# MLP and routing of a half in one stage, with the first choice of experts inside the MLP, and the shared experts inside the first expert stage

## What is computed

```
# layer 1, after the attention
x  = Q + out @ wo + bo
x  = x + gelu(layernorm(x) @ w1 + b1) @ w2 + b2           # MLP, width 512
z  = layernorm(x)                                          # rows for the mixture
scores = sigmoid(z @ gate_w.T)                             # 64 experts in 8 groups of 8
# the best 4 groups by the sum of their two best; in them the best 8 experts
rw = scores of the chosen / (their sum + 1e-20) * 2.5
routed = sum over e of rw[:, e] * mlp_e(z)                 # mlp_e: width 88
shared = (silu(z @ Sg.T) * (z @ Su.T)) @ Sd.T              # width 176 = 2 x 88
x = x + tanh(g_ffn) * (routed + shared)
```

## Time and profile before

| what | us |
|---|---|
| median of three runs | 1210.32 |
| profiled execution | 1209.28 |
| its span | 1207.1 |
| MLP and routing of half 0, about | 196 to 296 |
| MLP and routing of half 1, about | 461 to 554 |
| expert stage 0, TensorE | 554 to 702 |
| TensorE without work | 702 to 727.56 |
| expert stage 1, TensorE | 727.56 to 917 |
| layer 2 | 917 to 1207 |

### The profile page before, as it was taken

How to read it: one execution, slowest core, us unless ns; L and a number is a source line. 1 busy time by engine, 2 the same in 40 slices (tenths; PEclk the granted TensorE clock), 3 DMA queues, 4 the chain that set the end, 5 groups by cost and what they waited for, 6 DMA issues and landing times.

```text
span 1207.1 us, 20571 instructions
## 1 busy us (share of the span) xinstructions
PE 1079.1 (89%) x6232; PEld 742.7 (62%) x6232; DVE 837.1 (69%) x2982; ACT 680.1 (56%) x1192; POOL 539.2 (45%) x544
## 2 busy tenths in 40 slices
PE   5999998875999998778999928998988999999998
PEld 2556665643666665547999917897884444444443
DVE  6888886797888885876444404658665888888643
ACT  3556663342666654334666614556646677767775
POOL 0000000041777772043777777776643777772000
PEclk9999999986999999988999968999989999999999
DMA  9999000000111114005778626666654534554241
GB/s 280 312 285 343 37 1 1 1 1 2 51 53 52 53 54 115 1 1 161 232 245 251 218 88 197 200 197 179 193 161 176 193 93 161 203 202 165 96 161 59
DMA packets 104408, 165.15 MB, mean 137 GB/s; under 512 B 13423, under 2 KB 63063, under 8 KB 99673
## 3 DMA queue, kind: packets, MB, share of 16 engines
q1 hardware_dynamic: 87806, 130.39, 33.2%
q0 software_dynamic: 16512, 33.59, 9.5%
HBM read 94.46 MB, written 69.47 MB: 136 GB/s over the span
## 4 chain that ended last, share of the span: by engine, by line
PE 69%; DVE 19%; POOL 4%; ACT 4%; issue 3%; DMA 1%; SPq 0%; DVEq 0%; ACTq 0%; POOLq 0%
PE PS L1857 8%; PE PS L706 6%; PE PS L1874 6%; PE PS L696 6%; PE PS L1695 5%; PE PS L1685 4%; PE PS L1662 4%; PE PS L1678 4%; PE PS L1657 4%; PE PS L1851 3%; PE PS L1866 3%; PE PS L1670 2%; POOL sorted_rows L945 2%; PE PS L1751 2%; PE PS L1744 2%
## 5 line engine op out<-in xcount | busy, mean ns | idle before, releaser
L964 POOL DMA_INDIRECT sb_Y<-sorted_out,sb_POS x256 | 258.3, 1009 | 114.0 <-issue 68.9
L945 POOL DMA_INDIRECT sorted_rows<-sb_XR,sb_POS x256 | 247.2, 966 | 89.4 <-issue 79.4
L905 POOL TENSOR_TENSOR sb_A<-sb_A 88x512 f32<-88x512 f32 x16 | 21.3, 1349 | 293.3 <-ACT sb_A L1089 293.3
L1857 PE MATMUL PS<-sb_WGU,sb_A 128*128 x768 | 138.4, 324 | 4.6 <-ACT sb_A L1131 4.6
L706 PE MATMUL PS<-sb_A,sb_RT 128*128 128x512 f32 x256 | 131.8, 599 | 4.0 <-DVE sb_A L529 3.9
L1131 ACT ACTIVATE sb_A<-PS 128x512 f32<-128x512 f32 x96 | 57.3, 597 | 130.8 <-PE PS L1851 130.8
L529 DVE SCALAR_TENSOR_TENSOR sb_A<-sb_A,sb_RW 128x512 f32<-128x512 f32 x124 | 85.0, 689 | 60.9 <-ACT sb_A L378 60.3
L1857 PEld LDWEIGHTS PS<-sb_WGU,sb_A 128*128 128x128 f32 x768 | 120.5, 197 | 9.9 <-issue 9.8
L1584 DVE TENSOR_SCALAR sb_A<-PS 128x4 f32<-128x4 f32 x96 | 15.5, 161 | 150.7 <-ACT sb_A L1136 147.8
L696 PE MATMUL PS<-sb_WGU,sb_RT 128*128 128x512 f32 x224 | 115.7, 598 | 0.0
L372 ACT ACTIVATE sb_A<-PS,sb_A 128x512 f32<-128x512 f32 x128 | 87.3, 682 | 41.7 <-PE PS L696 40.6
(11 more groups left out here) (278 smaller groups left out, 2081.8 us busy)
## 6 DMA issues: line engine op xcount, KB each, us to landing
sb_RW<-routing SPq DMA_DIRECT2D x31, 1024.0 KB, 7.6
sorted_rows<-sb_RT SPq DMA_DIRECT2D x2, 12288.0 KB, 77.4
sb_A<-sorted_rows SPq DMA_DIRECT2D x96, 256.0 KB
sorted_out<-sb_A SPq DMA_DIRECT2D x96, 256.0 KB
sb_WGU<-in_wgu SPq DMA_DIRECT2D x1, 5664.0 KB, 60.9
sorted_rows<-sb_XR,sb_POS POOLq DMA_INDIRECT x256
sb_Y<-sorted_out,sb_POS POOLq DMA_INDIRECT x256
sb_RW<-in_wd SPq DMA_DIRECT2D x1, 2816.0 KB
```

Of the source, the lines that this page charges most:

```text
L945: pool.indirect_dma_start(out=xs[c], in_=XR[:, t, :], in_offset=None, out_offset=bass.IndirectOffsetOnAxis(ap=POS[:, b * TOPK + k:b * TOPK ...
L964: pool.indirect_dma_start(out=GBUF[r][:, k * D:(k + 1) * D], out_offset=None, in_=ys[c], in_offset=bass.IndirectOffsetOnAxis(ap=POS[:, b * ...
L1857: ins = mm(gu_bank[r % 2][:, t, 0:1 + 2 * EI], EXT[:, t * P:(t + 1) * P], WGU[:, e[t], :], start=True, stop=True)
```

## The change

On every engine `mlp(c)` and `route(c)` become one function (`ffn(c)` on TensorE and ScalarE, `mlp(c)` on VectorE). The rows of the first two groups are normalised and scored as soon as the MLP has finished with these groups, and their choice (`choose(c, 0)`) stands on VectorE between the MLP's third and fourth group. The scores of two groups leave PSUM by one Sigmoid of 128x512 in place of two of 128x256.

The first pieces of an attention (`begin`: transposes, query and key products and their squares for the first tile) are cut off, and for half 1 they stand inside the stage before. At the start of the kernel the same cut moves ScalarE's first roots behind the squares of the keys and the transposes' eviction of the second tile.

`chosen_scores` of half 0 moves into the attention of half 1; that of half 1 moves into step 1 of expert stage 0. `slot_counts` becomes shorter: its two operations of 128x1024 become operations of 128x64.

The shared experts leave routing and GpSimd. Steps 1 to 40 of expert stage 0 carry them, five steps to a group, eight groups (both halves): four steps with one matmul each, all into the one PSUM bank 7, and a fifth with the sixteen matmuls back into the same bank. ScalarE takes the Silu of the first and third, VectorE the product after the second and fourth, and the addition to `x` after the fifth.

The expert step has another order: `hT`, `T`, the shared matmul, `gu`, `down`. One semaphore (`e_a`) is raised after `hT` and `T`, one (`e_b`, in the listings `ex_gu_y`) after `gu` and `down`. The row's score is no longer folded into the hidden values (one operation of 128x352 in place of four of 128x88), but multiplies the result of `down` as it leaves PSUM, and this eviction (`y_out`) moves from ScalarE to VectorE. The hidden buffers are doubled. SyncE's waits and GpSimd's pace follow the two new semaphores.

GpSimd loses this function, which ran ahead of each half's scatter:

```diff
-            def shared(c):
-                for g in range(c * GC, (c + 1) * GC):
-                    sil, h = SIL[g % 2], SHH[g % 2]
-                    for n in range(2):
-                        pool.wait_ge(r_si, g * 2 + (n + 1))
-                        nc.gpsimd.tensor_tensor(h[:, n, :], sil[:, n, :], h[:, n, :], ALU.mult).then_inc(r_h, 1)
-                    pool.wait_ge(r_oe, g + 1)
-                    xg = X[:, g * G:(g + 1) * G, :]
-                    nc.gpsimd.tensor_tensor(xg, SHO[g % 2].rearrange("p (t d) -> p t d", t=G), xg, ALU.add).then_inc(r_x, 1)
```

Which steps carry shared work, and ScalarE: the cut in its attention, and its share of the shared experts in `experts(c)`:

```diff
+        def shared_step(c, k):
+            n = k - SHARED
+            return divmod(n, 5) if c == 0 and 0 <= n < 5 * (B // G) else None
...
-                qk_in(lo)
-                q_sq(lo)
+                if begin:
+                    if c:
+                        act.wait_ge(m_x, c * GC + 1)
+                    qk_in(lo)
+                    q_sq(lo)
+                    k_sq(lo)
+                    qk_in(lo + 1)
+                    return
                 roots(lo, 0)
-                k_sq(lo)
-                qk_in(lo + 1)
...
+                def shared(k, g, j):
+                    if j % 2 == 0 and j < 4:
+                        act.wait_ge(e_b, b_sig(c, k))
+                        act.wait_ge(r_h, 2 * g + j // 2)
+                        nc.scalar.activation(SIL, bank(7, 1, 0, EI), ACT.Silu).then_inc(r_si, 1)
```

VectorE, in `experts(c)`:

```diff
+                def shared(k, g, j):
+                    if j % 2:
+                        dve.wait_ge(e_b, b_sig(c, k))
+                        dve.wait_ge(r_si, 2 * g + j // 2 + 1)
+                        v.tensor_tensor(SHH[j // 2], SIL, bank(7, 1, 0, EI), ALU.mult).then_inc(r_h, 1)
+                    if j == 4:
+                        dve.wait_ge(e_b, b_sig(c, k))
+                        v.scalar_tensor_tensor(X[:, tiles(g), :], t3(bank(7)), TG[:, 1:2], X[:, tiles(g), :], ALU.mult,
+                                               ALU.add).then_inc(r_x, 1)
+
+                for k in range(-1, SS + 2):
+                    if 0 <= k - 2:
+                        y_out(k - 2)
+                    if k + 1 < SS:
+                        h(k + 1)
+                    if shared_step(c, k):
+                        shared(k, *shared_step(c, k))
+                    if not c and k == 1:
+                        chosen_scores(CHUNKS - 1)
```

TensorE, in `experts(c)`:

```diff
+                def shared(g, j):
+                    if j == 0:
+                        pe.wait_ge(r_x, g)
+                        if g == 0:
+                            pe.wait_ge(t_rout, CHUNKS * NRK)
+                    elif j < 4:
+                        pe.wait_ge(r_si if j % 2 else r_h, 2 * g + (j + 1) // 2)
+                    else:
+                        pe.wait_ge(r_h, 2 * g + 2)
...
+                for k in range(-2, SS + 2):
+                    if k <= SS:
+                        if 0 <= k - 1:
+                            ins = hT(k - 1)
+                        if k + 2 < SS:
+                            ins = T(k + 2)
+                        ins.then_inc(e_a, 1)
+                    if k + 2 < SS:
+                        experts_of[k + 2] = slot_experts(pe, c, k + 2)
+                    if shared_step(c, k):
+                        shared(*shared_step(c, k))
+                    if -1 <= k:
+                        if k + 1 < SS:
+                            ins = gu(k + 1, experts_of[k + 1])
+                        if 0 <= k - 2:
+                            ins = down(k - 2, experts_of.pop(k - 2))
+                        ins.then_inc(e_b, 1)
```

More of the change, by code:

```diff
@@ L236, in build @@
         e_ld = [sem(f"ex_load{i}") for i in range(4)]
-        e_t, e_te, e_gu, e_si, e_h, e_ht, e_hte, e_y, e_ye = (sem("ex_" + n) for n in (
-            "xT", "xT_out", "gu", "silu", "h", "hT", "hT_out", "y", "y_out"))
+        e_a, e_b, e_te, e_si, e_h, e_w, e_hte, e_ye = (sem("ex_" + n) for n in (
+            "xT_hT", "gu_y", "xT_out", "silu", "h", "score", "hT_out", "y_out"))
         e_st = [sem(f"ex_store{i}") for i in range(2)]
@@ L969, in _ @@
             for c in range(CHUNKS):
-                shared(c)
                 scatter(c)
@@ L981, in _, with attention @@
             nc.scalar.activation(TG[:], VEC[:, V_GATES:V_GATES + 4], ACT.Tanh).then_inc(gates, 1)
-            def attention(c):
+            def attention(c, begin=False):
                 lo, hi = chunk_tiles(c)
@@ L1118, in route @@
+                z_out(lo + GC - 1)
+                rows_out(0)
+                rows_out(1)
+                gelu(lo + GC - 1, range(0, 2))
+                scores(0)
+                gelu(lo + GC - 1, range(2, 4))
                 ranks(0)
                 ranks(1)
-                out(3)
+                rows_out(2)
+                rows_out(3)
+                scores(1)
+                if c + 1 < CHUNKS:
+                    attention(c + 1, True)
+                act.wait_ge(t_rank, c * NRK + 3)
@@ L1154, in experts @@
-                hT_out(0, 0)
-                def body(i, r, first=False):
-                    x_out(i + 2)
-                    silu(i + 1, (r + 1) % 2)
-                    hT_out(i, r % 2)
-                    y_out(i - 1, (r - 1) % 2, first)
-                body(1, 1, c == 0)
-                body(2, 2, c == 0)
-                if c == 0:
-                    with act.Fori(0, (SS - 8) // 4) as q:
-                        for r in range(4):
-                            body(q * 4 + (3 + r), 3 + r)
@@ L1168, in experts @@
-                for i in range(3 if c else 3 + (SS - 8), SS - 2):
-                    body(i, i % 4)
-                    if c:
-                        early(i)
-                silu(SS - 1, 1)
-                hT_out(SS - 2, 0)
-                y_out(SS - 3, 1)
-                hT_out(SS - 1, 1)
-                y_out(SS - 2, 0)
-                y_out(SS - 1, 1)
+                    act.wait_ge(e_a, a_sig(c, i - 2))
+                    if i >= 2:
+                        act.wait_ge(e_b, b_sig(c, i - 3))
+                    elif c:
+                        act.wait_ge(e_b, SIG)
@@ L1370, in attention @@
                         body(first, True)
-                    first += 1
+                    body(lo + 2)
+                    chosen_scores(c - 1)
+                    first += 2
                 S.loop(first, hi - 2, body, 10 if c + 1 < CHUNKS else 9)
@@ L1420, in mlp @@
                     dve.wait_ge(zeroed, 16 * CHUNKS)
-                for i in range(GC - 1):
-                    routed_z(c, i)
-                x(hi - 1)
+                routed_z(c, 0)
+                routed_z(c, 1)
+                x(lo + 2)
+                choose(c, 0)
+                x(lo + 3)
+                dve.wait_ge(m_z, hi)
+                tile_stats(slice(2 * G, TC))
+                routed_z(c, 2)
+                routed_z(c, 3)
+                if c + 1 < CHUNKS:
+                    attention(c + 1, True)
+                choose(c, 1)
             def routed_z(c, i):
@@ new lines, in experts @@
+                for k in range(-1, SS + 2):
[4 more added lines that the diff above has]
+                    if shared_step(c, k):
+                        shared(k, *shared_step(c, k))
+                    if not c and k == 1:
+                        chosen_scores(CHUNKS - 1)
+                    if c:
+                        n = k - 1
+                        if 0 <= n < 3 * TC and n % 3 == 1:
+                            add_rows(start + n // 3, n // 3 % 4)
+                        if 0 <= n < 3 * TC and n % 3 == 2:
+                            add_to_x(start + n // 3, start)
+                        early(k)
@@ L1628, in _ @@
             dve.wait_ge(gates, 1)
+            attention(0, True)
             for c in range(CHUNKS):
```

492 lines of the change are left out of this document (209 added, 283 removed).

## The result

Four runs of the changed kernel gave 1254.16 to 1257.22 us, median 1256.99; four of the kernel before 1208.93 to 1222.42, median 1210.26. The ratio is 1.036, with a 95% interval of 1.032 to 1.040. The profiled execution has a span of 1255.4 us, 48.3 more than before.

The account below looks back on a forecast made before the run. TensorE was taken to bound expert stage 0, VectorE the MLP and routing. Stage 0 +65, routing -14 and -13, stage 1 -6 and start +2.5 sum to +34.5 on 1209.3: 1243 us named, range 1213 to 1264.

Parts of the forecast that it names:

- the case: Whole kernel as computed, without a rival: 1226 to 1260 us, likeliest 1243, chance 0.60.
- The ring: Stage 0: shared matmuls wait for VectorE's product behind y_out; a group takes 26.4 us, +65 to stage 1's first transpose.
- The hole: After stage 0: TensorE's 25.84 us wait for the second scatter is filled; 6 us to stage 1's first transpose stay.
- Routing: MLP and routing on VectorE: -14 us in half 0, -13 in half 1; together between 20 and 37 gained.
- The slowed choices: Routing: VectorE's choices no longer run beside GpSimd's products; 8.2 us go in half 0, 3.9 in half 1.
- the late ranks: Routing of half 1: of the 7.08 us wait for ScalarE's copy of the ranks, 5.5 go.
- the counts and the sums of scores: Routing, each half: shorter slot_counts saves 1.8 us, and chosen_scores leaving the chain saves 3.1.
- Stage 1: Expert stage 1: more slack and doubled hidden buffers mean fewer TensorE stalls, -6 us, between -15 and +5.
- Start: Kernel start: ScalarE's first roots stand later, delaying the first queries and the first attention, +2.5 us, at least 0.
- the first (no ring): Stage 0: TensorE doesn't wait for shared results, a group costs 20.1 us, 50 us less in all: 1193; chance 0.11.
- The third (routing gives more): Both halves give 37 us instead of 27, stage 1 gives 15: 1225, or 1210 with the ring's low bound; chance 0.17.
- The second, a clock that falls in the shared steps: Stage 0: one slow step per group, 2.7 us in each of eight groups, 21 us: 1264; chance 0.12.

Follow-up runs that it names:

- run 11: Changed kernel with shared product first, first roots early, stage 1's loads early, layer 2 pieces a step later, and an own signal per shared matmul: 1201.81 us.
- run 8: Kernel before the change without the shared experts, everything else in its old order: 1195.13 us.
- run 9: run 1 with VectorE's first choice of each half moved behind the MLP's last group: 1222.97 us.
- run 1: Changed kernel with VectorE's shared product (or addition to x) put ahead of y_out in a step of stage 0: 1211.56 us.
- run 4: Changed kernel with ScalarE's first roots back in their old place at the kernel's start: 1249.81 us, 1242.31 to 1258.87 in four runs.
- run 2: Changed kernel with VectorE's shared product computed twice, the first time into a spare buffer: 1266.55 us.
- run 7: Changed kernel with twelve products of 88x512 per half put back on GpSimd, on spare buffers: 1270.05 us.

## Why the prediction was right, step by step

The direction and the case were right: 1257 lies in the range of 1213 to 1264, 14 us above the 1243 named. The ring, the term that decides, was right in its mechanism and its size; what is off by 14 us lies in other stages.

- **The ring in stage 0**: forecast +65 us from the first hT to the first transpose of stage 1; measured 236.9 - 173.5 = +63.4. A group was worked out at 26.4 and takes (738.06 - 554.83) / 7 = 26.2 us between the matmuls back of the first and of the last group. It holds step by step: a step behind ScalarE takes 4.22 us (4.2 worked out), one behind VectorE 5.48 (5.7), the one with the matmuls back 6.50 (6.6), except that one of these last took 8.16, at a lower clock (below). The estimate of 0.55 for the 128x352 product is 0.51 in the rows. One reading behind it was off without harm: the window of 556 to 720 takes in 18 us of the hole. In 556 to 702 TensorE is busy 143.30 of 146 us at full clock, so stage 0 was TensorE's even more than I said, and VectorE was idle for 78 us of it, not 96. Without the ring TensorE's own work was priced at 20.1 us a group, and run 11, which has no ring, takes 4 x 3.83 + 4.76 = 20.1.
- **The hole**: it is filled, as forecast. The way to stage 1's first transpose, priced at 6, is 7.2.
- **Routing**: forecast -14 and -13; measured 82.7 - 100.5 = -17.8 with +2.8 in the attention behind it, thus -15.0, and -12.3. That the totals fit is in part luck, since three terms were off and nearly cancelled. The slowed choices were right: 8.2 and 3.9 forecast, 8.4 and 4.1 by run 8's rows. With the late ranks (5.5) I had counted 17.6 for the leaving of the shared experts; run 8 has 25.4 for it, among other things because I had kept half 0's wait of 5.22 for TensorE. The moved choice, to which I had given no price of its own, is worth 12 (run 9 against run 1). Of the rest of the merge I expected a gain (the counts and the sums of scores 9.8, less 1.3 for the second logits), and it costs some 5 (run 9 against run 8, 173.0 - 168.3): VectorE now waits for the second Sigmoid in each half, 3.42 and 5.17 us in the changed kernel. In half 1:

```profile
514.01 0.69 DVE L1424 TENSOR_TENSOR sb_RT<-sb_RT,sb_ROWS 128x512 f32<-128x512 f32 x1 [5.17 <-ACT sb_RT L1086]
```

  25.4 + 12.4 - 4.7 is 33.1, what run 1 gained in its halves; the changed kernel gained 3 less, in half 1. The prediction also calls 27 us "VectorE's idle time", but its rows have 13.7 + 15.3 = 29.0 of that, and most of its 27 is work taken off VectorE.
- **Stage 1**: this step failed in its direction. I forecast -6 from more slack; the stretch from the first transpose to the last down grew by 1.1, which is no more than such stretches vary by (run 8, with the old order, has 190.4). TensorE is idle for 18.1 us of it before and after: the doubled buffers took no stall away in total. Its longest waits are for VectorE's pieces of layer 2. The wait of 3.82 is one of 5.24 after, in front of the same matmul, and y_out now stands in VectorE's queue behind those pieces:

```profile
925.09 1.96 PE L673 MATMUL PS<-sb_AW 32*77 32x128 f32 x8 [5.24 <-DVE sb_AW L473]
...
928.70 2.57 PE L1824 MATMUL PS<-sb_WGU,sb_A 128*128 x8
```

- **Layer 2**, not in my sum: +2.8. The clock in its first 20 us is 0.88 (above); the same stretch before had 1.00:

```profile
916.78:936.00 19.22, 19.22 (x72) 9.05 (x70) 6.30 (x10) 14.59 (x25) 12.20 (x12) 1.00 0.62 229
```

  A clock of 0.88 over 20 us is 2.4 us of work. What went before is the tail of stage 1, in whose steps TensorE waits for y_out. That the tail is the cause was not tried by itself.
- **Start**: forecast +2.5, measured +8.3. Of this 3.5 lie ahead of the second tile's first transpose (17.29 before, 20.82 after) and are not the change's: a load of constants landed 14.6 us after its issue instead of 11.0. The other 4.8 hold two things. TensorE, having waited for VectorE behind that load, did the first products of the keys at the slower clock (3.62 us instead of 1.88). The rest is the order of the roots, the term that I had; its mechanism is seen (run 4). In run 8, which has the old order and as late a load (the second tile at 21.39), that way takes 7.9 instead of 11.4, so the order is worth 3.4 there; over all profiles it is some 2.

The sum again: 34.5 forecast, + 5.8 at the start, + 7.1 in stage 1, + 2.8 in layer 2, and - 1.9 in routing and stage 0 together give the 48.3 measured.

Of the rivals, the first (no ring) is what runs 1 and 11 became by an edit, and the changed kernel wasn't. The third (routing gives more) didn't come: the halves gave 27, not 37.

The second, a clock that falls in the shared steps, came true at a small size. In the changed kernel the granted clock falls to 1.2 GHz once in stage 0, in the step of the third group's matmuls back:

```profile
608.91 2.57 PE L1824 MATMUL PS<-sb_WGU,sb_A 128*128 x8
611.27 1.37 PE L1841 MATMUL PS<-sb_RW,sb_A 88*128 x8
```

This gu takes 611.27 - 608.91 = 2.36 us instead of 1.2, and the step 8.16 instead of 6.50: 1.7 us a time, where I had 2.7 in each of eight groups. Runs 2, 4 and 7 have the ring too, and in them it falls six, five and two times in stage 0; in none of the nine profiles without the ring does it fall there at all. This accounts for what their stages 0 have more: run 4 is 6.7 us longer than the changed kernel (four falls more, 6.6), run 7 1.7 (one more), run 2 17.7 (9.6 of products, and five more). Their clocks in 545 to 730, first run 2, then run 4:

```profile
545.00:730.00 185.00, 146.48 (x940) 124.52 (x939) 69.22 (x193) 54.66 (x109) 94.55 (x100) 0.95 0.44 139
```

```profile
545.00:730.00 185.00, 152.47 (x988) 130.34 (x987) 65.34 (x192) 58.31 (x116) 100.39 (x106) 0.96 0.47 146
```

These rows agree with the rule of the Trainium skill named in the prediction ("TensorE: Matmul & The Clock Gate", section "A second HAM failure mode: psum-queue depth-cycling"): the falls come only in the kernels in which TensorE waits briefly in every group. But they come in few of the groups, not in each, and cost 1.7 us in the execution that was compared. The comparison by which the prediction placed the ring doesn't hold, though: its 20.1 of 26.4 us is a share of 0.76 and lies above both rows named beside it (0.73 and 0.74), not between them.

## What to carry to other kernels

Work that is pushed between the steps of a pipelined loop costs its own time only if its operands come back before the engine meets its next piece. If the helper's operation stands behind others that wait for the end of the step, the loop closes into a ring, and then an idle helper engine doesn't help: what counts is the order in its queue (45 us here) and which signal it waits for (7 us).

Before filling a hole, ask what else begins at its end: here loads that came 4 us earlier let stage 1 begin ahead of the gather, and TensorE stood 3.6 us longer in it. What else lengthened that stage, a lower clock, has no cause shown.

A merge of two stages should be priced by parts: here the work that left gave 25 us, the one block that moved 12, and the merge around them took some 5 back, a difference of single runs.

## What the runs showed that I had not expected

One load at the kernel's start landed between 10.0 and 15.1 us after its issue in the thirteen profiles, old order or new. With the clock that follows a late one, this moves the first attention by up to 9 us (23.1 to 32.2) between kernels that differ nowhere ahead of it or by one ScalarE block.

The clock fell in stage 0 in the four kernels with the ring alone, and not equally often: one, six, five and two times, 1.7 us each. Whether the ring also makes the whole time less steady is not shown: run 4 has 1242 to 1259 us in four runs, but the changed kernel 1254 to 1257 in four, and the kernel before, without a ring, 1208 to 1225 in thirteen.
